# Later units for the preparation of the next block's x in a gated cross-attention and MoE kernel

## The reference

```python
def _L0_xattn_ref(q, k, v, Wq, bq, Wk, bk, Wv, bv, Wo, bo):
    Q = (q @ Wq.T + bq).reshape(bs, sl, H, HD)        # H = 16, HD = 64
    K = (k @ Wk.T + bk).reshape(bs, sl, H, HD)
    V = (v @ Wv.T + bv).reshape(bs, sl, H, HD)
    score = jnp.einsum('bshd,bsgd->bshg', Q, K)
    weight = jax.nn.softmax(score, axis=-1)
    attn = jnp.einsum('bshg,bsgd->bshd', weight, V).reshape(bs, sl, nf)
    return attn @ Wo.T + bo
...
x = x + tanh(g_xattn[0]) * _L0_xattn_ref(_layernorm(x), ctx_2048, ctx_2048, ...)
x = x + tanh(g_ffn[0]) * _L0_ffn_ref(_layernorm(x), ...)
```

## Time and profile before

| | |
|---|---|
| median of 3 runs | 3112.35 us (3108.13 to 3113.08) |
| the profiled execution's own time | 3115.78 us |
| its span, first to last instruction | 3114.1 us |
| busy: PE, DVE, ACT, POOL | 2979.9, 2197.3, 1351.0, 1400.2 us |
| granted TensorE clock, mean | 0.986 |
| attention, one block | about 71 us |

### The profile page before, as it was taken

How to read it: one execution, slowest core, us unless ns; L and a number is a source line. 1 busy time by engine, 2 the same in 40 slices (tenths; PEclk the granted TensorE clock), 3 DMA queues, 4 the chain that set the end, 5 groups by cost and what they waited for, 6 DMA issues and landing times.

```text
span 3114.1 us, 62714 instructions
## 1 busy us (share of the span) xinstructions
PE 2979.9 (96%) x21264; PEld 1809.4 (58%) x21264; DVE 2197.3 (71%) x3798; ACT 1351.0 (43%) x2189; POOL 1400.2 (45%) x1326
## 2 busy tenths in 40 slices
PE   6999999999999996999999899999999999999996
PEld 5677777777777763444444445555555555555552
DVE  6677767777777777777777766666666665666663
ACT  5444444444444444111111125555555555555552
POOL 4222222222222213455555645666666665666663
PEclk9999999999999998999999999999999999999998
DMA  6333333433333336444444459999999999999996
GB/s 223 86 89 85 87 89 103 106 83 86 89 86 89 86 96 203 133 136 136 136 136 136 130 166 247 269 280 272 267 276 272 268 279 255 276 284 272 287 277 129
DMA packets 429405, 545.46 MB, mean 175 GB/s; under 512 B 226248, under 2 KB 324552, under 8 KB 429233
## 3 DMA queue, kind: packets, MB, share of 16 engines
q1 hardware_dynamic: 349360, 308.07, 33.2%
q0 software_dynamic: 79872, 235.06, 32.1%
HBM read 340.27 MB, written 203.88 MB: 175 GB/s over the span
## 4 chain that ended last, share of the span: by engine, by line
PE 80%; DVE 10%; issue 5%; DMA 2%; POOL 1%; ACT 1%; DVEq 0%; SPq 0%; POOLq 0%; ACTq 0%
PE eturn_ps L2130 7%; PE proj_ps L867 4%; PE proj_ps L869 4%; PE proj_ps L868 4%; PE proj_ps L913 4%; PE v_ps L2141 3%; PE v_ps L2140 3%; PE v_ps L2139 3%; PE g_ps L2140 3%; PE g_ps L2141 3%; PE g_ps L2139 3%; PE edown_ps L2158 3%; PE edown_ps L2157 3%; PE edown_ps L2156 3%; PE proj_ps L914 3%
## 5 line engine op out<-in xcount | busy, mean ns | idle before, releaser
L1926 POOL DMA_INDIRECT out<-outs,target x256 | 402.2, 1571 | 308.1 <-ACT outs L2017 248.0
L2040 DVE TENSOR_TENSOR ext_lo<-eturn_ps,ext_hi 128x1024 f16<-128x1024 f32 x254 | 311.1, 1225 | 262.3 <-ACT ext_hi L1977 259.3
L1892 POOL DMA_INDIRECT rows<-rows_dram,index x256 | 354.4, 1384 | 118.7 <-POOL index L1888 59.9
L1977 ACT ACTIVATE ext_hi<-eturn_ps 128x1024 f16<-128x1024 f32 x254 | 259.9, 1023 | 216.2 <-PE eturn_ps L2130 216.2
L867 PE MATMUL proj_ps<-ct_hi,wk_wv_hi 128*128 128x256 f16 x1024 | 282.2, 276 | 20.8 <-DVE wk_wv_lo L720 9.5
L867 PE MATMUL proj_ps<-xt,wq_wo_hi 128*128 128x256 f16 x1024 | 279.4, 273 | 4.0 <-DVE whole L696 3.1
L868 PE MATMUL proj_ps<-ct_lo,wk_wv_hi 128*128 128x256 f16 x1024 | 281.9, 275 | 0.0
L869 PE MATMUL proj_ps<-ct_hi,wk_wv_lo 128*128 128x256 f16 x1024 | 281.8, 275 | 0.0
L869 PE MATMUL proj_ps<-xt,wq_wo_lo 128*128 128x256 f16 x1024 | 279.1, 273 | 0.0
L868 PE MATMUL proj_ps<-xt,wq_wo_hi 128*128 128x256 f16 x1024 | 279.1, 273 | 0.0
L2017 ACT ACTIVATE outs<-edown_ps,weight 128x512 f32<-128x512 f32 x256 | 175.9, 687 | 236.7 <-PE edown_ps L2158 222.9
(11 more groups left out here) (206 smaller groups left out, 7308.8 us busy)
## 6 DMA issues: line engine op xcount, KB each, us to landing
ew_in<-w_up SPq DMA_DIRECT2D x64, 1024.0 KB, 7.7
ew_in<-w_down SPq DMA_DIRECT2D x64, 512.0 KB, 8.3
x_in<-x SPq DMA_DIRECT2D x16, 1024.0 KB, 6.1
v_dram<-vt SPq DMA_DIRECT2D x64, 256.0 KB, 2.1
late<-v_dram SPq DMA_DIRECT2D x32, 512.0 KB, 7.5
attn_dram<-attn SPq DMA_DIRECT2D x64, 256.0 KB, 2.1
a_in<-attn_dram SPq DMA_DIRECT2D x32, 512.0 KB, 4.1
rx_in<-x SPq DMA_DIRECT2D x32, 512.0 KB, 4.4
```

Of the source, the lines that this page charges most:

```text
L1892: pool.indirect_dma_start(out=rows[par][:, k, :], out_offset=None, in_=rows_dram, in_offset=bass.IndirectOffsetOnAxis(ap=index[:, par, k:k ...
L1926: pool.indirect_dma_start(out=out, out_offset=bass.IndirectOffsetOnAxis(ap=target[:, k:k + 1], axis=0), in_=outs[:, k, :], in_offset=None, ...
L1977: act.activation(xt_hi[e.base % 2][:, :, k * P:(k + 1) * P], turned_ps(e, k), ACT.Copy).then_inc(xt_hi_made, 1)
L2040: dve.tensor_tensor(xt_lo[e.base % 2][:, :, cols], turned_ps(e, k), xt_hi[e.base % 2][:, :, cols], ALU.subtract).then_inc(xt_lo_made, 1)
```

## The change

The table that says in which unit of a block the next block's x is worked on gets later entries for all jobs but the moments:

```diff
-X_AT = {"stats": (3, 4), "norm": (5, 6), "hi": (6, 11), "lo": (7, 12), "turn": (8, 13)}
+X_AT = {"stats": (3, 4), "norm": (9, 12), "hi": (12, 17), "lo": (14, 18), "turn": (15, 19)}
 X_AT_FIRST = {"stats": (9, 10), "norm": (11, 12), "hi": (13, 17), "lo": (14, 18), "turn": (15, 19)}
```

## The result

The changed kernel takes **3088.16 us** (median of 4 runs, 3087.53 to 3092.24). The kernel before took 3110.24 us (4 runs, 3107.14 to 3113.08) in the same comparison: a ratio of 0.9935, 95% interval 0.9923 to 0.9948. The medians lie 22 us apart; by the ratio the gain is 20 us (16 to 24). The profiled execution took 3088.35 us, with a span of 3086.3.

What follows compares the result with a forecast made beforehand. PE bounds the kernel, waiting at `weigh(1)` for DVE's `split_probs` in blocks 1 to 14. Profiled 3115.78 less 19.5 gives 3096.3; the runs' median lies 3.4 below the profiled execution, so 3092.9 us, range 3087 to 3104.

Steps and rivals of the forecast that it cites:

- The gain: At `weigh(1)`, unit 10 of blocks 1 to 14: PE's wait of 1.48 us goes to 0, together 19.5 us.
- The other bound: Pair 1's L762 on DVE: earliest end 565.56, from 568.31 less 2.75 us of moved `norm` and `lo`.
- The margin: At `weigh(1)`: pair 1's L762 ends 0.1 to 1.3 us before PE wants it at 566.89.
- Rival 1: At `weigh(1)`: part of the wait stays through POOL and ACT; half left gives 3102.6 us; chance 0.14.
- `weigh(2)`, next to be late: At unit 15, pair 2: margin 0.97 to 1.85 us after the change, so no new wait.
- Rival 2: Wait moves to `weigh(2)`, both `norm` now between pair 1's and 2's splits; at 2.4 us later, 3112 us; chance 0.07.
- The second transpose: Behind `store_v(1)` on SP: lands 2.5 to 3.1 us before the next block's first Q matmul; cost 0.
- Rival 3: Second transpose lands late, each next block's first Q unit waits; at 10 us landing, +15.5 us, 3127.9; chance 0.07.
- ACT's `hi`: Tile 1's `hi`, after pair 3's exponentials, comes 2.6 us after the first transpose has landed at 587.8.
- `lo` of tile 1 beside `split_v`: On DVE in the V units: `lo` takes 1.44 us as in block 0, fitting the idle time with 0.11 left.
- `lower` at 0.61: POOL's L475 of pair 1, without `norm` beside it, takes 0.61 instead of 1.01 us.

Runs made afterwards that it cites:

- the filler: Changed kernel with four more bn_stats, results unread, on DVE at unit 5 of blocks 1 to 14, ahead of L762: 3110.13 us, ratio 1.0.
- the two half changes: Changed kernel with both `norm` back at units 5 and 6: 3093.85 us; kernel before with only tile 1's `norm` moved, unit 6 to 9: 3099.21 us.
- block 0's table: Changed kernel with block 0's units in all blocks (moments at 9 and 10, `norm` at 11 and 12, first `hi` at 13): 3106.81 us, ratio 0.999.
- The late transposes: Changed kernel with the second transpose at unit 21 instead of 19, behind the third V store: 3141.66 us, ratio 1.01.
- the first experiment: Changed kernel with both `norm` back at units 5 and 6, `hi`, `lo` and `turn` left late: 3093.85 us, ratio 0.9948.

## Why the prediction was right, and where not

**The gain: right, by its mechanism.** The forecast let L762 end at 565.92, which is 565.92 - 559.19 = 6.73 us after L740's start and comes from block 15's row less its wait for PE; 6.76 are measured. The other bound, 565.56, took the moved rows at their full lengths, 2.75 us, and was too early: 9.12 - 6.76 = 2.36 us left the chain. Part of the difference is that rows of DVE overlap at their ends (L740 ends at 559.19 + 0.42 = 559.61, the `norm` behind it starts at 559.53). The wait is 0 in all fourteen blocks, and the filler brings one back. The margin, forecast as 0.1 to 1.3, is 0.65 to 1.08. Rival 1 (a part stays) is what the two half changes show: 0.16 to 0.37 with the `norm` early, 0.59 to 0.80 with one `norm` late.

**Its size: a little small.** 19.5 us of waits gave 20.8. A wait is counted from the end of the matmul before it, but without a wait the next matmul starts before that end: `weigh(1)` began 558.82 - 558.61 = 0.21 us after the last start of unit 9, and with the wait 568.37 - 566.61 = 1.76, which is 1.55 and not 1.48 more. Fourteen times 0.07 is 1.0. In the timeline before:

```profile
566.61 0.27 PE L869 MATMUL proj_ps<-ct_hi,wk_wv_lo 128*128 128x256 f16 x1
```

So 1.3 of the 4.7 us between 3092.9 and 3088.16 are the gain. Another 2.1 are the base: the kernel before took 3110.24 us beside the changed one (3109.4 to 3110.7 in the other comparisons), not the 3112.35 that I took. 3110.24 - 20.8 = 3089.4, and the last 1.3 are within what single runs differ by. The range held narrowly: 3088.16 is 1.2 us above its lower end, which allowed 1.6 us for a quicker machine and nothing for a gain above the waits.

**`weigh(2)`, next to be late: right.** Its margin was forecast as 0.97 to 1.85 and is 1.27 to 1.69. Rival 2 was no idle thought: block 0's table makes it true, 1.1 to 1.3 us at each `weigh(2)`. The change escapes it because the moments stay early, at units 3 and 4, and only the `norm` stand between the splits.

**The second transpose: right.** Forecast 2.5 to 3.1 us to spare, measured 3.0 in the block shown (2.9 to 3.4 in blocks 2 to 15). Rival 3's price was too low. I counted a landing time of 10 us as the bad case and the wait alone as its price. The late transposes landed within 7 us, but over a quarter came on top of their waits (53.3 for 40.6), most of it in a slower clock behind the longer ones.

**ACT's `hi`: right, with an error in its sum.** 582.6 + 5.0 is 587.6 and not 587.8, so the working gives 2.8 us to spare. The limit of 5.0 for a landing didn't hold, as first transposes of a block took up to 5.9 in the changed kernel. `hi` of tile 1 had 1.9 to 3.2 us all the same. In the block shown the first transpose landed near 574.73 + 4.3 = 579.0, ahead of 582.22:

```profile
574.73 1.77 SPq L334 DMA_TRANSPOSE xt<-xw  x1
...
582.22 1.04 ACT L558 ACTIVATE xw<-x_in 128x1024 f16<-128x1024 f32 x1
```

**`lo` of tile 1 beside `split_v`: wrong.** The prediction took 1.44 from block 0 and called the rule of the Trainium skill (SBUF — State Buffer, Who interferes with whom) "far smaller" in effect than its full form. In all fourteen blocks that changed, `lo` of tile 1 takes 1.79 to 1.80 us. In the block shown it starts at 584.21, `split_v` ends at 583.76 + 1.16 = 584.92, and 584.92 + 1.18 = 586.10 is about its end, 586.00. It waits out the rest of `split_v`, as that rule has it: VectorE and GpSimd share a port pair, and the one that has it shuts the other out. Block 0's 0.26 was merely a shorter overlap: `split_v` ended at 94.73 + 1.16 = 95.89, and 95.89 + 1.18 = 97.07 is about `lo`'s end, 95.53 + 1.44 = 96.97. It cost nothing because, as the working said, only margin hangs on it: L706 follows without idle time, and PE doesn't wait.

**`lower` at 0.61: right**, and by the first experiment worth little by itself.

## What to carry to other kernels

Where the bounding engine waits at one place, read the releasing engine's queue from the last input to the release, and add up what stands there on other business. The gain is that sum or the wait, whichever is less (here 2.36 against 1.48 us a block); what is over is margin. Then do the same for the next release, as the moved work lands in front of it; other units in the same table decided between 22 us faster, no clear change and 32 us slower. A moved step brings its partners on other queues with it: a moment late on VectorE held up a `lower` behind its deviation on GpSimd.

## What the runs showed of the hardware

- A wait can cost more than its length. Behind the five waits of 3.9 to 4.8 us for a transpose the granted clock was 0.50 to 0.67 over the next 4.2 us, and behind the 5.20 us in block 15 it was 0.64 over 5.4 us; behind eight of nine waits of 1.8 to 2.2 us it stayed at 1.00, and at 0.65 behind the ninth. Behind the 1.48 us of the kernel before it stayed at 1.00, or the gain would have been larger than the waits. The rows of block 15 in the changed kernel, then those behind the 1.48 us of the kernel before:

```profile
1135.80:1141.20 5.40, 5.32 (x38) 2.65 (x40) 5.20 (x11) 2.85 (x4) 0.00 (x0) 0.64 0.53 182
```

```profile
568.30:573.70 5.40, 5.33 (x83) 4.75 (x84) 5.11 (x14) 2.12 (x7) 0.00 (x0) 1.00 0.41 52
```

- A transposing DMA took 4.2 to 5.0 us to land in the kernel before; up to 5.9 in the changed one, and up to 6.9 with the second turn at unit 21. Those of over 5.5 us come in every other block from block 4 on, in the changed kernel always as the first of the two. More is not moved beside them: with the second turn at unit 21, the late one issued at 538.43 had 171 GB/s in its flight of 6.36 us, the punctual one issued at 466.50 had 235 in its 4.42. (The windows behind the waits, above, start when these have landed.) What sets the late ones apart is a packet of an "instruction" queue, q8: in the two traces together each of the 19 transposes of 4.9 us or more has one in its flight, and none of the 41 others, of 4.4 at most. The line of the late flight, which the view of the punctual one doesn't have (packets, MB, share of the 16 engines):

```profile
q8 instruction: 1, 0.02, 0.9%
```

That this packet is the cause is not shown: no run moved it, and other experiments have a few punctual transposes with one.
- GpSimd's small steps stretch beside a `norm` of VectorE as well: `lower` took 1.01 us there, and 0.61 or 0.62 in the rows above that have no `norm` beside them.
